# Products for two tiles at a time in a transformer layer: the q, k and up weights each meet 256 columns instead of 128, and the turned tiles are loaded earlier in SyncE's queue

## The reference, cut to what matters

```python
x = hidden                      # [8, 2048, 256]
# first half: causal linear attention over chunks of 128 positions
h = layernorm(x)
q, k, v = h @ w_q.T, h @ w_k.T, h @ w_v.T
sq, sk = elu(q) + 1, elu(k) + 1
A = (sq @ sk.T) * tril                       # per chunk
num = A @ v + sq @ S_kv;  den = A.sum(-1) + sq @ z
S_kv += sk.T @ v;  z += sk.sum(0)            # carried from chunk to chunk
out = g * (sq @ memory) / (sq @ memory_norm) + (1 - g) * num / den
x = x + layernorm(out @ w_o.T)
# second half: a dense MLP plus product-key experts (4 heads, 1024 experts, 8 chosen per head)
h = layernorm(x)
dense = silu(h @ W_up.T) @ W_down.T          # 256 -> 1024 -> 256
route = h @ (W_q, keys)                      # top 8 of sums of two halves' scores
w = silu((h @ down_embed.T) * softmax(top 8 scores))   # kept for the chosen experts alone
x = x + layernorm(dense + w @ up_embed)
```

## Time and profile before

| | us |
|---|---|
| median of 3 runs (lowest, highest) | 2856.78 (2856.33, 2860.16) |
| the profiled execution's own time | 2860.13 |
| its span | 2858.4 |
| TensorE busy in the span | 2829.4 |
| ScalarE, VectorE, GpSimd busy | 2525.0, 2424.2, 2055.1 |

### The profile page before, as it was taken

How to read it: one execution, slowest core, us unless ns; L and a number is a source line. 1 busy time by engine, 2 the same in 40 slices (tenths; PEclk the granted TensorE clock), 3 DMA queues, 4 the chain that set the end, 5 groups by cost and what they waited for, 6 DMA issues and landing times.

```text
span 2858.4 us, 48065 instructions
## 1 busy us (share of the span) xinstructions
PE 2829.4 (99%) x14724; PEld 2294.9 (80%) x14724; DVE 2424.2 (85%) x6125; ACT 2525.0 (88%) x3618; POOL 2055.1 (72%) x2460
## 2 busy tenths in 40 slices
PE   8899999999999999999999999999999999999999
PEld 6688788878888888888788878888888788788877
DVE  5888888888888888888888888888888888888886
ACT  5888998899888989888998898888989888998997
POOL 3677777777777777777777777777777777777674
PEclk9999999999999999999999999999999999999999
DMA  4576667766766766676667766666767676667664
GB/s 120 140 174 166 166 172 172 167 169 169 170 165 170 171 168 167 169 173 167 165 172 173 167 168 170 168 166 170 171 168 167 169 173 166 167 171 171 151 152 120
DMA packets 450053, 471.58 MB, mean 165 GB/s; under 512 B 234883, under 2 KB 384516, under 8 KB 449796
## 3 DMA queue, kind: packets, MB, share of 16 engines
q0 software_dynamic: 52832, 199.77, 36.1%
q1 hardware_dynamic: 396964, 268.74, 31.1%
HBM read 137.37 MB, written 131.20 MB: 94 GB/s over the span
## 4 chain that ended last, share of the span: by engine, by line
PE 95%; ACT 1%; DVE 1%; issue 1%; POOL 1%; DMA 1%; SPq 0%; POOLq 0%; DVEq 0%; ACTq 0%
PE banks L684 89%; PE banks L828 4%; PE banks L810 2%; POOL sums L532 0%; DMA g_parts<-w_way 0%; DVE w_blocks L1117 0%; DVE prob L1109 0%; DMA wexp<-wexp 0%; ACT prob L979 0%; PE banks L619 0%; PE banks L627 0%; PE banks L641 0%; DMA w_way<-w_blocks 0%; PE banks L661 0%; PE banks L698 0%
## 5 line engine op out<-in xcount | busy, mean ns | idle before, releaser
L532 POOL TENSOR_TENSOR sums<-scores 128x1024 f32<-128x1024 f32 x512 | 1002.3, 2037 | 76.0 <-ACT scores L1018 76.0
L518 POOL TENSOR_TENSOR rstd<-var_eps,minus_half 128x1 f32<-128x1 f32 x512 | 501.9, 980 | 43.0 <-ACT y_sq L928 15.3
L684 PEld LDWEIGHTS banks<-xn2T,wupT 128*128 128x128 f32 x4096 | 484.0, 188 | 9.4 <-DVE state L1171 3.0
L684 PE MATMUL banks<-xn2T,wupT 128*128 128x128 f32 x4096 | 486.2, 274 | 2.1 <-DVE state L1171 2.1
L684 PE MATMUL banks<-deT,xn2T 128*128 128x512 f32 x1024 | 484.4, 596 | 2.4 <-DVE picked L1064 2.0
L684 PE MATMUL banks<-ue,gT 128*128 128x256 f32 x2048 | 462.8, 379 | 0.3 <-ACT gT L957 0.3
L684 PE MATMUL banks<-wdownT,hT 128*128 128x256 f32 x2048 | 462.8, 379 | 0.2 <-ACT y_sb L1014 0.2
L684 PEld LDWEIGHTS banks<-wdownT,hT 128*128 128x128 f32 x2048 | 389.0, 190 | 56.8 <-issue 3.0
L684 PEld LDWEIGHTS banks<-ue,gT 128*128 128x128 f32 x2048 | 388.7, 190 | 52.7 <-ACT gT L957 0.7
L570 POOL TENSOR_TENSOR wexp<-wexp,w_last 128x1 f32<-128x1 f32 x127 | 131.6, 1036 | 385.1 <-ACT z_last L1007 385.1
L684 PEld LDWEIGHTS banks<-deT,xn2T 128*128 128x128 f32 x1024 | 191.9, 197 | 130.9 <-issue 121.2
(11 more groups left out here) (162 smaller groups left out, 6661.2 us busy)
## 6 DMA issues: line engine op xcount, KB each, us to landing
wexp<-wexp POOLq DMA_DIRECT2D x127, 1024.0 KB, 9.1
wexp<-wexp POOLq DMA_DIRECT2D x127, 512.0 KB, 4.7
w_way<-w_blocks SPq DMA_DIRECT2D x127, 512.0 KB, 2.6
g_parts<-w_way SPq DMA_DIRECT2D x508, 128.0 KB, 4.9
xn_way<-xn_blocks SPq DMA_DIRECT2D x248, 128.0 KB, 1.8
x_in<-_attn_hidden_states_dram SPq DMA_DIRECT2D x128, 128.0 KB, 2.2
out_dram<-x_out SPq DMA_DIRECT2D x128, 128.0 KB, 1.8
xn1T<-xn_way SPq DMA_DIRECT2D x500, 32.0 KB, 2.2
```

The costliest lines, as they stand in the source:

```text
L518: return nc.gpsimd.tensor_tensor(rstd[:, n, m:m + 1], var_eps[:, n, m:m + 1], minus_half[:, :], ALU.pow)
L532: return nc.gpsimd.tensor_tensor(sums[:, k, :, :], scores[:, k, 0:XIN].unsqueeze(2).broadcast_to([P, XIN, NKEYS]), scores[:, HEADS + k, :] ...
L684: last = nc.tensor.matmul(out, lhs(c), rhs(c), start=(start and c == 0), stop=(stop and c == chunks - 1))
```

## The change

From tile 6 on (`PAIRED`), one stationary block of W_q, W_k or W_up meets the columns of two tiles at once. `two_tile_q_or_k` and `up` make products 256 columns wide. The products of two steps are dealt out anew: in an even tile's step TensorE makes k for the tiles t and t+1, in an odd one's q for t+1 and t+2; in an even tile's step the up products of the first four blocks of hidden units for both tiles, in the odd one's those of the last four. Tiles 126 and 127 keep single up products, and tile 127's step has neither q nor k products. Per tile there are as many columns, and half as many matmuls.

For this `xn1T` and `xn2T` get four buffers (`TURNED`), `hT` four, `sig` one buffer for k and two for q. A tile's first norm, its way out and its gather run one step earlier from tile 5 on (`ahead`, `AHEAD` = 4). In SyncE's queue the gather of xn2 stands right behind the writing out of the expert weights, and sk out and the gather of xn1 follow it; the gather of the expert weights comes behind them. The first pair's q goes through bank 0 in tile 6's step, with a Relu, an Exp and a sigma of its own.

```diff
+    PAIRED = 6
+    AHEAD = 4
+    TURNED = 4
...
-        xn1T = sb("xn1T", [P, 2, P, DC])
-        xn2T = sb("xn2T", [P, 2, P, DC])
+        xn1T = sb("xn1T", [P, TURNED, P, DC])
+        xn2T = sb("xn2T", [P, TURNED, P, DC])
...
-        sig = sb("sig", [P, 2, 2 * DC, P])
+        sig = sb("sig", [P, 3, DC, 2, P])
...
+        def two_tiles(b):
+            return b.rearrange("p (c t n) -> p c t n", t=2, n=P)
...
+        def ahead(t, stage):
+
+            old, new = t[stage], t[stage - 1]
+            if old is not None and old < AHEAD:
+                return old
+            return new if new is not None and new > AHEAD else None
+
+        def up_done(step):
+            return step - 9
+
+        def hidden_at(t):
+            return t // 2 * 2 + 2 if paired_up(t) else t + 1
+
+        def paired_up(t):
+            return PAIRED <= t < LATE
...
+            def xn1_in(x):
+                moved(sp, s_xn1_blocks_out, x, 1, TILES, EARLY)
+                wait(sp, s_v_in_psum, x + 1 - TURNED)
+                gather(xn1T[:, x % TURNED, :, :].rearrange('p (i t) c -> p i (t c)', t=BLOCK), xn1_way[x % 2, :, :], s_xn1_blocks_in[x % 2])
...
+                if t[8] is not None:
+                    if EARLY <= t[8] < LATE:
+                        moved(sp, s_xn2_blocks_out, t[8], 1, LATE, EARLY)
+                        wait(sp, s_up_0_in_psum, t[8] - 2)
+                        gather(xn2T[:, t[8] % TURNED, :, :].rearrange('p (i t) c -> p i (t c)', t=BLOCK), xn2_way[t[8] % 2, :, :], s_xn2_blocks_in[t[8] % 2])
...
+            def up(t, half):
+
+                if not paired_up(t):
+                    for k in range(4):
+                        ic = 4 * half + k
+                        last = product(u_ps[half][:, k * P:(k + 1) * P], DC, lambda c: wupT[:, c, ic * P:(ic + 1) * P],
+                                       lambda c: xn2T[:, t % TURNED, :, c])
+                else:
+                    first = t // 2 * 2 % TURNED
+                    for k in range(2):
+                        ic = 4 * (t % 2) + 2 * half + k
+                        last = product(two_tiles(u_ps[half])[:, k, :, :], DC, lambda c: wupT[:, c, ic * P:(ic + 1) * P],
+                                       lambda c: xn2T[:, first:first + 2, :, c])
+                return last
+
+            def two_tile_q_or_k(dst, w, t):
+                for ec in range(DC):
+                    last = product(two_tiles(dst)[:, ec, :, :], DC, lambda c: w[:, c, ec * P:(ec + 1) * P],
+                                   lambda c: xn1T[:, t % TURNED:t % TURNED + 2, :, c])
+                return last
...
+                    if paired_up(u) and u % 2 == 0:
+                        moved(pe, s_xn2_blocks_in, u + 1, BLOCKS, LATE, EARLY)
+                    wait(pe, s_state_ready, u + 2, KEPT)
+                    wait(pe, s_hidden_1_ready, u)
+                    up(u, 1).then_inc(s_up_1_in_psum, 1)
+                    wait(pe, s_hidden_0_ready, u)
+                    up(u, 0).then_inc(s_up_0_in_psum, 1)
...
+                    elif t[7] % 2 == 1:
+                        moved(pe, s_xn1_blocks_in, t[7] + 1, BLOCKS, TILES, EARLY)
+                        moved(pe, s_xn1_blocks_in, t[7] + 2, BLOCKS, TILES, EARLY)
...
+                    elif t[7] % 2 == 0:
+                        two_tile_q_or_k(qk_ps, wkT, t[7]).then_inc(s_qk_in_psum, 1)
+                    elif t[7] < TILES - 1:
+                        two_tile_q_or_k(qk_ps, wqT, t[7] + 1).then_inc(s_qk_in_psum, 1)
...
+            def hidden(t, half):
+
+                s_up, s_ready = ((s_up_0_in_psum, s_hidden_0_ready), (s_up_1_in_psum, s_hidden_1_ready))[half]
+                act.wait_ge(s_up, t + 1)
+                if not paired_up(t):
+                    nc.scalar.activation(flat(hT[:, t % 4, 4 * half:4 * half + 4, :]), u_ps[half][:, :], ACT.Silu).then_inc(s_ready, 1)
+                else:
+                    ic = 4 * (t % 2) + 2 * half
+                    wait(act, s_y_hidden_in_psum, pair_of_free(t))
+                    nc.scalar.activation(hT[:, pair_of(t):pair_of(t) + 2, ic:ic + 2, :].rearrange("p t i n -> p i t n"),
+                                         two_tiles(u_ps[half]), ACT.Silu).then_inc(s_ready, 1)
+
+            def pair_of_free(t):
+                return t // 2 * 2 - 2
...
+            def sigma(dst, exp, relu):
+                return nc.vector.scalar_tensor_tensor(dst, two_tiles(exp), 1.0, two_tiles(relu), ALU.min, ALU.add)
```

More of the change, by code:

```diff
@@ L331, in pipeline, with sig_k, sig_q, q_buffer @@
                      STAGES + SLOTS <= step < KEPT)
+        def sig_k(t, c):
+            return sig[:, 0, c, t % 2, :]
+        def sig_q(t, c):
+            return sig[:, q_buffer(t), c, t % 2, :]
+        def q_buffer(t):
+            return 1 if t < PAIRED else 1 + ((t - PAIRED) // 2 + 1) % 2
+        def pair_of(t):
+            return t // 2 * 2 % 4
+        def ahead(t, stage):
[9 more added lines that the diff above has]
+            return PAIRED <= t < LATE
         def y_bank(t):
@@ L711, in body @@
                         turn_wdown(0, 0)
-                    if t[10] == TILES - 3:
+                    if u == TILES - 3:
                         turn_xn('xn2', xn2, s_xn2_ready, LATE)
-                    if t[10] == TILES - 2:
+                    if u == TILES - 2:
                         turn_xn('xn2', xn2, s_xn2_ready, LATE + 1)
-                    wait(pe, s_state_ready, t[10] + 2, KEPT)
-                    for k in range(4):
-                        ic = 4 + k
-                        last = product(u_ps[1][:, k * P:(k + 1) * P], DC, lambda c: wupT[:, c, ic * P:(ic + 1) * P],
-                                       lambda c: xn2T[:, t[10] % 2, :, c])
@@ L721, in body @@
-                    last.then_inc(s_up_1_in_psum, 1)
-                    if not steady:
-                        wait(pe, s_hidden_0_ready, t[10])
-                    for k in range(4):
-                        ic = k
-                        last = product(u_ps[0][:, k * P:(k + 1) * P], DC, lambda c: wupT[:, c, ic * P:(ic + 1) * P],
-                                       lambda c: xn2T[:, t[10] % 2, :, c])
-                    last.then_inc(s_up_0_in_psum, 1)
+                    if paired_up(u) and u % 2 == 0:
+                        moved(pe, s_xn2_blocks_in, u + 1, BLOCKS, LATE, EARLY)
@@ L777, in body @@
                     moved(pe, s_xn2_blocks_in, t[9], BLOCKS, LATE, EARLY)
-                    product(sc_ps[:, :], DC, lambda c: xn2T[:, t[9] % 2, :, c], lambda c: route[:, c, :]).then_inc(s_route_scores_in_psum, 1)
+                    product(sc_ps[:, :], DC, lambda c: xn2T[:, t[9] % TURNED, :, c], lambda c: route[:, c, :]).then_inc(s_route_scores_in_psum, 1)
                     if t[9] == 0:
@@ L793, in body @@
                     if t[7] >= BATCH:
[L794 removed]
+                        product(num_ps, DC, lambda c: sig_q(t[7], c), lambda c: state[:, seq_of(t[7]), c, :], stop=False)
                     if t[7] == 0:
@@ L1164, in body @@
                                                    ALU.is_ge, ALU.mult).then_inc(s_head_0_selected, 1)
-                if t[3] is not None:
-                    dve.wait_ge(s_x_stats, t[3] + 1)
-                    nc.vector.bn_aggr(mv[:, LN_X, t[3] % 2, :], stats[:, LN_X, t[3] % 2, :]).then_inc(s_x_moments, 1)
+                if t[3] == AHEAD:
+                    if AHEAD - 1 <= EARLY:
+                        dve.wait_ge(s_early_ps, TURN['xn1', AHEAD - 2] + 1)
+                    dve.wait_ge(s_x_rstd, AHEAD)
+                    xn1_made(AHEAD - 1)
+                    dve.wait_ge(s_xn1_ready, AHEAD)
+                if t[4] == AHEAD:
+                    xn1_turned(AHEAD)
+                x = ahead(t, 3)
+                if x is not None:
+                    x_moments(x)
                 if t[8] is not None:
```

238 lines of the change are left out of this document (144 added, 94 removed).

## The result

Measured side by side, the changed kernel takes 2875.59 us (median of 4 executions, 2873.20 to 2879.03) and the kernel before 2856.59 (4, 2856.33 to 2860.16): a ratio of 1.0065, 95% interval 1.0047 to 1.0082. It is slower by 0.65%, where 1.1% faster was forecast; the time lies outside the range. The profiled execution took 2873.3 us with a span of 2871.6, 13.2 more than the span before.

The account below looks back on a forecast made before the run. TensorE's own work was taken as the bound. From the profiled 2860.1 us, 32.4 of pace off and 1 for ramp and end gave 2828.7; the median, 3.35 lower, was 2825.5 (ratio 0.989), range 2819 to 2845.

Parts of the forecast that it names:

- What bounds the kernel: TensorE's unbroken stream of columns, 21.88 us per step; ScalarE and VectorE run close behind with small slacks.
- Rival 3: VectorE's or ScalarE's loop takes over, giving back 0 to 0.15 us per step: 2826 to 2844 us; chance 0.12.
- The pace: Up, q and k on TensorE: 24 records of 256 columns at 0.216 us each, 0.27 us less per step.
- the 0.004 that an up record costs above its share: Narrow up record's surplus on TensorE: once per record, for its weight load, or per column; gain 0.27, 0.17 or 0.08 us per step.
- rival 2: TensorE's extra cost stays per column: gain only 0.06 to 0.08 us per step, about 2849 to 2851 us; chance 0.08.
- SyncE's queue: Reordered gathers land in time: xn2 with 4 us of cover, xn1 issued before its need; cost nothing.
- rival 4: xn2's gather meets GpSimd's 1 MB DMA and lands 0.8 us late per pair: 2873 us or far more; chance 0.08.
- a step that is uneven: Named sign, in TensorE's steps, that the prediction is wrong altogether; the step was forecast at 21.6 us.
- The added waits on TensorE: Up products' new waits for the tile before's hidden units and, every second time, xn2: taken as 0.
- the table load that waits: ScalarE's Silu table load in even tiles waits for the dense down product, starting 0.5 us late: cost nothing.
- The ramp: First pair's extra Relu, Exp and sigma and reordered first norms: +1 us, bounds -2 to +4, including the end.
- The slower case: The whole kernel becomes slower than before, by a late xn2 only: chance 0.06.

Follow-up runs that it names:

- Experiment 9: The changed kernel with a wide product's columns kept in one piece and sk_blocks written out behind the gather of xn1T: 2834.05 us, ratio 0.9918.
- experiment 6: The changed kernel with GpSimd's two adding DMAs cut to 32 columns of each head: 2859.38 us, ratio 0.9993.
- experiment 7: The changed kernel with sk_blocks written out behind the gather of xn1T instead of ahead of it: 2862.69 us, ratio 1.0012.
- experiment 3: The changed kernel with the gather of xn1 moved ahead of the gather of xn2 in SyncE's queue: 3115.86 us, ratio 1.0895.

## Why the prediction was wrong

**What bounds the kernel** was read rightly: TensorE's columns, and the slack of VectorE and ScalarE. Experiment 9 gives 21.60 us per step, as the forecast had it, and leaves their waits near where the prediction put them. Rival 3 did not come.

**The pace: the step that failed first.** I split the 0.004 that an up record costs above its share into "once per record, or for its weight load" or "per column for the spacing (24 x 0.008 less, a gain of 0.08)", and doubled the narrow record's surplus to price the second case at 0.224. Both costs were there, and they don't add up. The narrow record shows the one that goes with its narrowness (0.1116 dense) and hides nearly all of the spacing's; the wide one shows 0.011 of spacing. The end that I had named, "0.227 per wide record, no gain", was the truth, and I had given it 0.08 of chance by way of rival 2. The argument "a cost per column would be a cost of reading, and 3% is odd for that" carried no number; and `sig` at 0.110, from four records of 0.44 us, was too coarse a row to tell 0.109 from 0.112. This term measured 0.02 us per step (21.86 against 21.88) instead of 0.27: 30 of the 32 us never came. The Trainium skill (SBUF — State Buffer, "Door 1: The DMA port swizzle") has an f32 stride of up to four elements read at full bandwidth; the trace here disagrees, with 0.227 at two and 0.449 at four against 0.216 at one.

**SyncE's queue: the step that gave the sign.** For xn2T it was right: issued in front of the adding DMA, landing in 2.2 us (forecast 2.6), some 4 us of cover; rival 4 did not come for xn2T. That rival 4's price, 2873 us, is near the measured time is chance: it was worked out for the other transfer and from another delay. But of xn1T I wrote "needed at 1528.3, against a gather issued by 1521 to 1524. Cost nothing". That sets an issue against a need and leaves the landing out. With the 7.3 us of the earlier trace rows, measured behind the adding DMA, it was 1528.3 to 1531.3 against 1528.3. The trace of before says it closer still: the adding DMA, issued at 1519.05, lands at 1528.10, and the four of xn2T, issued from 1522.08 to 1526.35, land at 1528.7 to 1529.6, just after it. The change had made the two gathers change roles: before, xn2T stood behind that DMA at 5.4 us and xn1T landed in 2.2; now xn1T stands there. I had priced this traffic for the transfer that left it and not for the one that entered it. Measured: 0.23 us in each of 53 steps and 2.0 in the last ones, 14 us; experiment 6 shows the cause and experiment 7 the size of the margin, half a microsecond. The Trainium skill (DMA: Bandwidth & Descriptors, "Queues, rings and completion order") has each DMA engine take turns between its queues a packet at a time. That the two queues meet in the engines fits the fourth issue's 1.9 us without the adding DMA's bytes and 7.5 with them; why it lands only with the whole of that DMA, no run here shows.

**The two together.** For the profiled execution the forecast was 2828.7 and the time 2873.3. Of the 44.6 us between them, 30 are the pace and 14 the waits for xn1T. One sign of being wrong that the prediction had named came true, "a step that is uneven".

**The rest.** The added waits on TensorE for `hidden_1_ready` and `hidden_0_ready`, and the table load that waits, cost nothing, as forecast (the wait ahead of the load in the changed kernel is 32.1 us over 52 times, 0.6 at most, and no step with k is longer than before). The ramp was +0.8 (+1).

**The chances.** The two steps were treated as unlikely extremes, and each had a row that spoke for it: the unexplained 0.004 of the up record, and the 5.4 to 7.3 us behind the adding DMA. The slower case was 0.06, for one transfer only.

## What to carry to other kernels

A record's surplus over its share of columns has several parts that may hide one another: before widening records, measure the wide one with the operand as it will really lie. When a queue is put in a new order, write for every transfer in it its issue, its landing by the row of its new place, and its need. Where several issues make one tile, take the landing of the last: a median over all of them fell from 5.9 to 1.9 us here while the last was in only 0.9 us earlier. The place behind a large transfer of another engine is a price that someone pays, and it should be one whose result is wanted last. A slack that is there because of the order isn't spare when the order changes.

## What the runs showed of the hardware

- The moving operand's spacing costs TensorE, for 256 columns of f32: 0.216 us in one piece, 0.227 at spacing two, 0.339 at three, 0.449 at four, 0.460 at eight. At 128 columns, one piece 0.1116 and spacing two 0.1137.
- A 32 KB gather on SyncE's queue whose issue starts up to 0.5 us behind that of a 1 MB accumulating DMA of GpSimd lands in 1.8 us (medians, here and below). One issued 1.3 to 2 us behind it takes 7.0 to 7.6 us, and lands up to 0.9 us after that DMA. About 1 us behind it, a gather takes 5 us, and 7.4 to 7.8 with runs of 128 bytes instead of 256. With the accumulating DMA cut to 32 KB all of these land in 1.8 to 2.1 us.
- TensorE's granted clock can fall behind a short idle stretch: in experiment 3 it was 0.69 for the 5.2 us after 2.8 us of idle time, which cost 1.6 us on top of the wait, and 44 of 51 idle stretches of 2.5 to 3.7 us had a stretch at 1.2 GHz behind them. An idle stretch of 2.1 us near the end had one behind it in the changed kernel and none in experiment 6.
